# A graph network kernel: the seam scores of 25 windows gathered for two windows at a time, and moved to their places by one more transfer

## The reference

```python
Wh = einsum('ni,hio->hno', x, W)
e_l = einsum('hno,ho->hn', Wh, a_l);  e_r = einsum('hno,ho->hn', Wh, a_r)
e = leaky_relu(e_l[:, src] + e_r[:, dst], 0.2) + log(clip(edge_weight, 1e-8))
alpha = exp(e.T - segment_max(e.T, dst)[dst])
alpha = alpha / (segment_sum(alpha, dst)[dst] + 1e-8)
out = segment_sum(alpha[:, :, None] * Wh.transpose(1, 0, 2)[src], dst) + bias
```

## Time and profile before

| | us |
|---|---|
| median of three timed executions | 8844.25 |
| lowest, highest | 8837.06, 8844.64 |
| the profiled execution's own time | 8821.84 |
| its span, first to last instruction | 8820.0 |

### The profile page before, as it was taken

How to read it: one execution, slowest core, us unless ns; L and a number is a source line. 1 busy time by engine, 2 the same in 40 slices (tenths; PEclk the granted TensorE clock), 3 DMA queues, 4 the chain that set the end, 5 groups by cost and what they waited for, 6 DMA issues and landing times.

```text
span 8820.0 us, 167686 instructions
## 1 busy us (share of the span) xinstructions
PE 6004.0 (68%) x48672; PEld 5105.3 (58%) x48673; DVE 3830.5 (43%) x9102; ACT 2410.1 (27%) x7270; POOL 1701.7 (19%) x1781
## 2 busy tenths in 40 slices
PE   2777799999999789999999904343434434444346
PEld 2666687878788689999999902232222222222224
DVE  7999888888888521111122202222222222222224
ACT  3666655555555311100011101111111111111112
POOL 1000000000000100000000064444444444443430
PEclk9999999999999889999999956666666666666667
DMA  6777788888888746666666621111111111111110
GB/s 212 294 295 295 296 326 322 326 331 331 323 326 328 260 156 261 266 264 261 263 256 248 198 47 32 34 32 34 32 34 32 34 32 33 33 33 32 34 31 17
DMA packets 420634, 1542.51 MB, mean 175 GB/s; under 512 B 77499, under 2 KB 108229, under 8 KB 368588
## 3 DMA queue, kind: packets, MB, share of 16 engines
q1 hardware_dynamic: 354388, 1405.92, 42.1%
q0 software_dynamic: 58784, 129.00, 6.2%
q10 hardware_dynamic: 7186, 4.22, 0.2%
HBM read 797.39 MB, written 743.08 MB: 175 GB/s over the span
## 4 chain that ended last, share of the span: by engine, by line
PE 55%; another core or an unknown queue 18%; DVE 10%; issue 9%; ACT 3%; ACTq 2%; DMA 2%; POOL 0%; SPq 0%; DVEq 0%; POOLq 0%
PE psum L1211 20%; PE psum L1166 12%; PE psum L1458 7%; PE psum L1131 7%; PE psum L1436 5%; DVE field L1698 4%; ACT field L1081 1%; ACT field L945 1%; ACTq L931 1%; PE psum L1456 1%; DVE work L2027 1%; DVE work L2034 1%; DVE field L1691 1%; PE psum L1157 0%
## 5 line engine op out<-in xcount | busy, mean ns | idle before, releaser
L1166 PE MATMUL psum<-field 128*128 128x200 bf16 (+1 forms) x14112 | 2067.2, 273 | 54.2 <-DVE field L1698 46.0
L945 ACT COPY field<-psum x4704 | 1670.5, 417 | 1121.8 <-PE psum L1166 1020.0
L870 POOL DMA_INDIRECT field<-head_table,cmp x1563 | 1497.3, 958 | 2000.3 <-PE psum L1458 1537.6
L1211 PE MATMUL psum<-field 128*128 128x128 f32 x14406 | 1789.3, 284 | 0.0
L1211 PEld LDWEIGHTS psum<-field 128*128 128x128 f32 x14406 | 1764.7, 190 | 0.0
L1698 DVE TENSOR_TENSOR field<-field 128x1176 bf16<-128x1176 bf16 x2352 | 1651.8, 765 | 0.0
L1456 PE MATMUL psum<-zero_b 128*128 128x2 bf16 x1611 | 289.8, 180 | 1717.8 <-ACT field L1081 1303.1
L1456 PEld LDWEIGHTS psum<-zero_b 128*128 128x128 bf16 x1611 | 171.9, 107 | 1894.0 <-issue 1873.9
L1166 PEld LDWEIGHTS psum<-field 128*128 128x128 bf16 x14112 | 1056.6, 99 | 337.7 <-issue 57.1
L1081 ACT COPY field<-psum x1611 | 433.6, 269 | 2784.1 <-remote 1629.5
L2084 DVE TENSOR_SCALAR params<-iota,cmp 128x128 f32<-128x128 f32 x1616 | 340.6, 286 | 1510.1 <-PE psum L1458 1170.5
(11 more groups left out here) (316 smaller groups left out, 3740.9 us busy)
## 6 DMA issues: line engine op xcount, KB each, us to landing
adj<-field SPq DMA_DIRECT2D x1764, 400.0 KB, 4.1
field<-adj SPq DMA_DIRECT2D x294, 1600.0 KB
X<-adj SPq DMA_DIRECT2D x49, 1600.0 KB, 7.6
work<-adj SPq DMA_DIRECT2D x49, 1600.0 KB, 7.6
field<-head_table,cmp POOLq DMA_INDIRECT x1563
field<-in_edge_attr SPq DMA_DIRECT2D x4, 3072.0 KB, 23.8
head_table<-field ACTq DMA_DIRECT2D x49, 68.0 KB, 1.6
tile_rows<-field SPq DMA_DIRECT2D x1, 3328.0 KB, 19.1
```

Source lines behind the costliest of these rows:

```text
L870: pool.indirect_dma_start(out=rows3[:, (i * WIN + t) * ROW3:(i * WIN + t + 1) * ROW3], out_offset=None, in_=head_table, in_offset=bass.Ind ...
L945: act.copy(evac[:, :, bass.ds(place, HALF)], build_banks[:, bass.ds(bank, NSEG * SEG)].rearrange("p (w c) -> p w c", w=ARRAYS)).then_inc(p ...
L1166: mm = pe.matmul(build_banks[:, bass.ds(cur[j % ROUND], end - first)], hot, pr[:, first:end], start=False, stop=True, skip_group_check=True)
L1211: mm = pe.matmul(ps_y[slot], source[:, hi, :], adj_in[slot][h].rearrange("p (g c) -> p g c", c=HALF)[:, :, at:at + 2], start=(hi == 0), st ...
```

## The change

Two windows lie side by side on the 128 partitions: the even window's 64 tiles on partitions 0 to 63, the odd window's on 64 to 127. `dst0` and `right0` get the shape for it, one column for each of 13 pairs (`TCOLS3`); `right0` keeps a second place in each column. GpSimd gathers 13 times 128 rows in place of 25 times 64. The scans read partitions 0 to 63 alone, so SyncE moves the odd windows' scores from partitions 64 to 127 to partitions 0 to 63 in one more DMA, behind its loads for windows 0 to 2, and VectorE waits for that DMA in place of the gathers. The indices take two loads in place of one. A window's column is where it was, so what the scans read is unchanged.

```diff
-        right0 = sb("right0", [WIN, TCOLS3 * HALVES, HEADS3])
-        dst0 = sb("dst0", [WIN, TCOLS3 * HALVES], I32)
+        right0 = sb("right0", [P, TCOLS3, HALVES, HEADS3])
+        dst0 = sb("dst0", [P, TCOLS3], I32)
@@ SyncE, behind the loads for windows 0 to 2
+            sp.wait_ge(right0_loaded, 16 * TCOLS3)
+            sp.dma_start(right0[0:WIN, :, 1, :], right0[WIN:P, :, 0, :]).then_inc(right0_moved, 16)
@@ GpSimd, early
-            pool.dma_start(dst0[:, :].rearrange("p (w a) -> p w a", a=1),
-                           strided(dst_pad, 1, [P, WIN], [WEDGES, TCOLS3 * HALVES], [1, 1]),
-                           allow_slow_non_contiguous=True).then_inc(dst0_loaded, 16)
+            for half in range(HALVES):
+                pp = slice(half * WIN, (half + 1) * WIN)
+                pool.dma_start(dst0[pp, :].rearrange("p (c a) -> p c a", a=1),
+                               strided(dst_pad, half * WEDGES + 1, [P, WIN], [HALVES * WEDGES, TCOLS3], [1, 1]),
+                               allow_slow_non_contiguous=True).then_inc(dst0_loaded, 16)
@@ GpSimd, before the rows of window 0
-            pool.wait_ge(dst0_loaded, 16)
+            pool.wait_ge(dst0_loaded, 16 * HALVES)
             pool.wait_ge(right0_ready, 1)
             pool.wait_ge(right_stored, 16)
-            for w_ in range(WINDOWS):
-                pool.indirect_dma_start(out=right0[:, w_, :], out_offset=None, in_=right_table,
-                                        in_offset=bass.IndirectOffsetOnAxis(ap=dst0[:, w_:w_ + 1], axis=0),
+            for c in range(TCOLS3):
+                pool.indirect_dma_start(out=right0[:, c, 0, :], out_offset=None, in_=right_table,
+                                        in_offset=bass.IndirectOffsetOnAxis(ap=dst0[:, c:c + 1], axis=0),
@@ VectorE
-                c.then(dve.memset(right0[:, :, :], 0.0))
+                c.then(dve.memset(right0[:, :, :, :], 0.0))
-            dve.wait_ge(right0_loaded, 16 * WINDOWS)
+            dve.wait_ge(right0_moved, 16)
             def right0_of(w, n):
-                return right0[0:n, w, :] if isinstance(w, int) else right0[0:n, bass.ds(w, 1), :].rearrange("p a h -> p (a h)")
+                by_window = right0[0:n, :, :, :].rearrange("p c i h -> p (c i) h")
+                return by_window[:, w, :] if isinstance(w, int) else by_window[:, bass.ds(w, 1), :].rearrange("p a h -> p (a h)")
```

More of the change, by code:

```diff
@@ L436, in build @@
         right0_loaded = sem("right0_loaded")
+        right0_moved = sem("right0_moved")
         tab_loaded = [sem(f"tab_loaded{i}") for i in range(DEPTH)]
```

## The result

| | before | after |
|---|---|---|
| executions | 22 | 22 |
| median, us | 8841.49 | 8828.47 |
| lowest to highest, us | 8831.65 to 8855.18 | 8815.13 to 8840.38 |
| the profiled execution's own time, us | 8821.84 | 8824.65 |

The ratio after to before is 0.9984, with a 95% interval of 0.9978 to 0.9991: 0.16% less, 13.0 us between the medians and 13.6 between the means (8842.2 and 8828.6). The interval in microseconds is 8 to 19. It lies wholly on the side of faster, and under the 0.2% that I had set as the border.

What follows compares the result with a forecast made beforehand. GpSimd's back-to-back issue of indirect DMAs, from the table's landing, was taken as the path. Gathers save 15.0 us, other parts cost 0: 8844.25 - 15.0 = 8829.2 us, range 8814 to 8846.

Steps and rivals of the forecast that it cites:

- The gathers: GpSimd ahead of window 0's rows: 13 gathers take 16.3 to 16.4 us instead of 31.40, saving 15.0 on the path.
- a distance of 1.25 to 1.27: Sign of being right: microseconds between seam gathers on GpSimd, with first row gather 16.3 to 16.5 us behind the first.
- near 2.2: Sign of being wrong: distance in microseconds between seam gathers on GpSimd's line 857.
- What is late next: Window 0's table loads on SyncE: landed by 5087, GpSimd needs them at 5091.0; nothing new late, 4 us to spare.
- The move: SyncE's new DMA before VectorE's seam scores: lands in 4.3 us (2.3 to 17.5), covered by window 0's row gathers; cost 0.
- The indices: GpSimd's index load at 76 us becomes two: at most 0.99 us more, covered by 39.58 us of idleness; cost 0.
- The tie to the end of the 128 gathers: Window 0's steps on ScalarE and TensorE wait for the first 128 row gathers' end; second copy within 2 us of it.
- From there to the end: End of the 128 row gathers to the last instruction: same time as before, within 17 us.
- The sum: Whole kernel: 15.0 us saved from a median of 8844.25, giving 8829.2 us, 0.17% less.
- The cost by rows: Rival at the seam gathers: cost goes with rows, 13 take 28.7 us, only 2.7 won, 8841.5; chance 0.05.
- VectorE late: Rival at window 0's seam scores: VectorE held until GpSimd's run ends, only 9.8 us won, 8834.5; chance 0.06.
- The clock: Rival in the windows: TensorE's granted clock falls, kernel slower than before, priced at 8869; chance 0.06.

Runs made afterwards that it cites:

- The kernel with half the gathers: Kernel before with only its first 13 of 25 seam gathers, 64 rows each, later windows' seam scores left out: 7199.39 us against 7213.7.
- fifty more: Kernel before with 50 more seam gathers of 64 rows, into unused places, ahead of window 0's rows: 7268.16 us against 7205.34.
- eight more in every window: Kernel after with 8 more seam gathers of 128 rows ahead of each window's row gathers, 200 in all: 7456.68 us against 7205.34.

## Why the prediction was right, and where its size was off

**The gathers.** The mechanism was right and the term a little mis-sized. I took 13 gathers at 1.256 to 1.263 us, 16.3 to 16.4 us; they took 17.07, 1.313 each, and the saving is 14.33 us in place of 15.0. I took the price of 128 rows from the row gathers, which are busy for 0.955 us; seam gathers with 128 rows are busy for 1.004. The kernel with half the gathers shows that the rows do it and not the count of gathers (0.952 with 64), and gathers into another tile, `bsum`, say the same: 0.945 in the median with 64 rows (fifty more) and 1.005 with 128 (eight more in every window). A row gather with as many rows is still 0.05 us shorter. It differs in its piece, 544 bytes against 16, in the table read, and in that the seam gathers ask for a `bounds_check` and the row gathers don't; which of them it is was not tried. The prediction compared a seam gather of 64 rows with a row gather of 128; the two forms differ by other things besides, which offset the cost of the rows and hid it. The test "a distance of 1.25 to 1.27" and "16.3 to 16.5 us" failed by that much, and "near 2.2" for the rival by far more. On the rule of the Trainium skill, Perfetto Trace Analysis, section "DMA Instruction — SWDGE (GPSIMD)", that the profiled time runs to the last descriptor written: twice the rows added 0.06 us to 0.95, so these runs agree that the number of descriptors shows, and show how little it weighs.

**What is late next.** Right. The last load was issued by 5088.13, and GpSimd's first row gather follows the last seam gather with 0.30 us of issue, no wait.

**The move.** Right in the sum, with a smaller size. SyncE was released 2.23 us behind the last gather (I had 2.3), and the move landed 2.38 us behind its issue, where I had 4.3: the lower end. I had weighed it by its count of pieces between a small gather and the store of 6272 pieces to memory; 832 pieces from partition to partition took the time of one small transfer. The Trainium skill, page DMA: Bandwidth & Descriptors, section "🔬 Anatomy of one DMA — SWDGE (gpsimd) path", fits 2.0 us and bytes over 436,000 a microsecond for one DMA, though for GpSimd's way of issuing. For these 13 KB that is an estimate of 2.03, near the 2.38; for the store of 98 KB it is 2.2, and the traces have 17.5 and 19.2. There the measurement decides: small pieces to memory are not priced by their bytes. The kernel without the move shows the cost of nothing directly.

**The indices.** Right. The timeline of GpSimd after has both loads in one row, and the idle time that covers them behind it:

```profile
75.89 1.60 POOL L807 DMA_DIRECT2D dst<-dst_pad  x2
...
116.84 0.96 POOL L816 DMA_INDIRECT field<-tile_rows,step_t_i  x1 [39.35 <-DMA tile_rows<-field]
```

They are busy for 1.60 us together, 0.61 more than the one; the cover shrank from 39.58 to 39.35.

**The tie to the end of the 128 gathers.** It held in the slower executions: they end at 5255.26 + 0.95 = 5256.21, 161.1 us behind the first (I had 161.3), and ScalarE's second copy starts 1.28 us behind that. It is no law of the program, though. In the 7200 us executions the second copy comes 6.06 us behind the first, 59 us ahead of that end. The prediction needed only that whatever bounds the windows follows GpSimd's first row gathers, and it does in both.

**From there to the end.** I allowed 17 us of scatter. The profiled pair has 3552.7 us before (8820.0 - 5267.30) and 3566.6 after (8822.8 - 5256.21), 13.9 more, within it. The 22 executions of each have 13.0 us between the medians, where a price of 13.9 us would have left next to nothing of the saving, and in the other sets the same change gives 14.5. So it is scatter in the main; a price of a few microseconds would not be seen in the interval of 8 to 19.

**The sum.** 8829.2 was forecast and 8828.47 measured, which flatters it: the median of the kernel before went from 8844.25 with 3 executions to 8841.49 with 22. The saving was 15.0 by forecast, 14.3 by the trace's stretch, and 13.0 to 13.6 by the executions.

**The rivals.** The cost by rows: some 6% of it is there (0.7 of 12.3 us, 0.06 a gather). VectorE late: it started 4.6 us behind the last gather, not at the end of the run; fallen. The clock: 0.64 over the same length of the windows in both; fallen.

## What to carry to other kernels

Where one engine issues small indirect transfers back to back on the path, price them by the number of instructions, about 1.26 to 1.31 us each here; more rows in each are almost free (0.06 us for 64 more of 16 bytes), and one more transfer to put things in their places is free while another queue and a long run of work cover it. To check a change worth 0.2%, compare the stretch it touches in the two traces and the medians of many executions; the ends of two profiled executions had the wrong sign here. And before trusting which engine bounds a stage, look whether it does so in every set of executions: this stage had two.

## What the runs showed of the hardware that was not expected

- One program had two levels, 8841 us and 7205 to 7214 us. The first five milliseconds are nearly alike: the first seam gather comes at 5074.58 and 5078.06 in the two slower traces, and at 5038 to 5060 in the ten faster ones. Then a window takes 147 to 153 us in the one (226 for the first) and 80 to 82 in the other, the last two aside. It parts in the softmax of window 0, where the same work takes 21.34 us against 12.46, and so ahead of the first steps. In the slower level a wait that ends when GpSimd's run of gathers ends (56.25 us on ScalarE, 41.47 on TensorE) stands where the faster one has 6.06. The granted clock of the windows was 0.64 against 0.78, at different shares of busy TensorE (1440 of 3448 us, 1167 of 1800). What sets the level was not found, since each set had but one of them; three chips were of the faster, and that the chip decides is neither shown nor ruled out.
- In the faster level a gather has no idle beside it but 0.30 us of issue, so that GpSimd, 24% busy over the span, is the bound of the last two milliseconds. In the chain of waits by engine it stood at 0% in the slower level, beside 18% for "another core or an unknown queue". Here, in the kernel before, it stands at 14% and that entry is gone:

```profile
PE 56%; POOL 14%; issue 10%; DVE 10%; ACT 3%; DMA 3%; ACTq 2%; SPq 1%; DVEq 0%; POOLq 0%
```

- 832 pieces of 16 bytes from 64 partitions to 64 others landed 2.38 us behind their issue (5096.05 to 5098.43) and 2.40 us in the other set, where 6272 pieces of 16 bytes to memory took 17.5 to 19.2 us.
